# A two-layer Mamba scan kernel: a tile's finished sum leaves PSUM in one VectorE instruction behind the scan, in place of two halves around it

## The reference

```python
def step(h, inp):
    x_t, dt_t, B_t, C_t = inp
    dA = jnp.exp(dt_t[:, :, None] * A)
    h = dA * h + dt_t[:, :, None] * B_t[:, None, :] * x_t[:, :, None]
    y = jnp.einsum('bds,bs->bd', h, C_t)
    return (h, y)
...
return y * _silu(z) @ W_out
```

## Time and profile before

| | us |
|---|---|
| median of 3 runs | 2131.67 |
| profiled execution | 2132.49 |
| its span | 2130.5 |
| busy: GpSimd (POOL) | 1938.7 |
| busy: VectorE (DVE) | 1829.3 |
| busy: TensorE (PE) | 1819.0 |
| busy: ScalarE (ACT) | 1163.3 |

### The profile page before, as it was taken

The page is one execution under the profiler, slowest core; times in us unless marked ns, Lnnn a source line. Parts: engine busy times, 40 slices in busy tenths (PEclk is TensorE's granted clock), DMA queues, the critical chain, the costliest instruction groups (busy, mean ns, idle before and its releaser), DMA issues. The chain is left out here.

```text
span 2130.5 us, 16128 instructions
## 1 busy us (share of the span) xinstructions
PE 1819.0 (85%) x4474; PEld 699.1 (33%) x4474; DVE 1829.3 (86%) x1110; ACT 1163.3 (55%) x1206; POOL 1938.7 (91%) x852
## 2 busy tenths in 40 slices
PE   5798789798899899789889889879989988987777
PEld 2233233333333333233333323323333333333322
DVE  2889887877799997997898997998889999799994
ACT  2756464655755745735655744744575574453331
POOL 0999989797899999999999999899899999999996
PEclk9799899999999999999999999999999999989997
DMA  3667556555566776775675785676566677667673
GB/s 83 206 222 185 188 179 189 156 202 189 143 208 204 206 221 205 198 216 191 192 207 197 218 208 204 219 194 211 172 193 208 204 203 217 215 201 213 223 211 94
DMA packets 124454, 415.01 MB, mean 195 GB/s; under 512 B 18556, under 2 KB 22924, under 8 KB 124364
## 3 DMA queue, kind: packets, MB, share of 16 engines
q1 hardware_dynamic: 124364, 413.98, 64.5%
HBM read 403.48 MB, written 6.29 MB: 192 GB/s over the span
## 5 line engine op out<-in xcount | busy, mean ns | idle before, releaser
L861 POOL TENSOR_TENSOR ring<-ring,c_ring 128x1024 f32<-128x1024 f32 x576 | 1344.4, 2355 | 116.9 <-DVE ring L817 104.5
L495 PE MATMUL y_ps<-ring,wp 128*128 128x512 f32 x2304 | 1184.6, 629 | 79.5 <-POOL ring L861 51.0
L817 DVE TENSOR_TENSOR_SCAN ring<-a_ring,b_ps 128x1024 f32<-128x1024 f32 x392 | 895.6, 2285 | 34.1 <-ACT a_ring L624 2.5
L495 PEld LDWEIGHTS y_ps<-ring,wp 128*128 128x128 f32 x2304 | 445.2, 199 | 574.4 <-issue 387.2
L817 DVE TENSOR_TENSOR_SCAN ring<-b_ps,b_ring 128x1024 f32<-128x1024 f32 x184 | 416.6, 2272 | 52.1 <-POOL b_ring L855 24.0
L784 DVE TENSOR_TENSOR b_ps<-u_ab,b_ps 128x1024 f32<-128x1024 f32 x240 | 291.1, 1213 | 101.1 <-PE b_ps L483 88.9
L624 ACT ACTIVATE a_ring<-delta_ab,wp 128x1024 f32<-128x1024 f32 x240 | 271.8, 1140 | 176.9 <-DVE ring L817 176.3
L855 POOL TENSOR_TENSOR b_ring<-u_ab,b_ring 128x1024 f32<-128x1024 f32 x144 | 339.2, 2355 | 0.1
L617 ACT ACT_TABLE_LOAD x186 | 238.6, 1283 | 84.6 <-PE bank L518 36.4
L624 ACT ACTIVATE b_ps<-delta_ab,wp 128x1024 f32<-128x1024 f32 x144 | 160.4, 1115 | 221.2 <-DVE ring L817 220.7
L624 ACT ACTIVATE a_ring<-delta_m,wp 128x1024 f32<-128x1024 f32 x152 | 173.6, 1143 | 152.0 <-DVE ring L817 151.7
(11 more groups left out here) (75 smaller groups left out, 930.4 us busy)
## 6 DMA issues: line engine op xcount, KB each, us to landing
c_ring<-c_rows SPq DMA_DIRECT2D x384, 512.0 KB, 4.4
c_ring<-c_rows SPq DMA_DIRECT2D x384, 256.0 KB, 4.2
b_ring<-b_rows SPq DMA_DIRECT2D x144, 512.0 KB, 5.6
b_ring<-b_rows SPq DMA_DIRECT2D x80, 256.0 KB, 5.3
out<-io SPq DMA_DIRECT2D x16, 192.0 KB, 3.1
io<-x SPq DMA_DIRECT2D x6, 384.0 KB, 6.7
b_in<-parts SPq DMA_DIRECT2D x36, 64.0 KB, 2.1
dt_in<-parts SPq DMA_DIRECT2D x72, 24.0 KB
```

Source lines behind the costliest of these rows:

```text
L495: nc.tensor.matmul(half(y_ps[:, :], j), ident, half(ring[:, g % RING, :], j), start=(n == 0), stop=(n == NS - 1)).then_inc(g_summed, 1)
L817: nc.vector.tensor_tensor_scan(out=h, data0=a, data1=b, initial=0.0, op0=ALU.mult, op1=ALU.add).then_inc(h_ready, 1)
L861: nc.gpsimd.tensor_tensor(r, r, c_ring[:, g % C_RING, :], ALU.mult).then_inc(g_ready, 1)
```

## The change

VectorE's order in a step becomes scan, take, ahead, jobs. The take is one instruction over all 1024 columns, behind the scan of the fourth step of the next tile; it waits for both half-sums of the last step. y_taken counts one per tile instead of two, and its users' values follow: the first half-sum and the second half-sum of a tile's first step both wait for the whole take of the tile before. The last tile is taken in one instruction as well.

```diff
--- before.py
+++ after.py
@@ -73,7 +73,7 @@
 ACT_ORDER = ("ahead_a2", "ahead_a", "jobs")
 SP_ORDER = ("ahead_b", "ahead_c", "jobs")
 POOL_ORDER = ("ahead_b", "product", "jobs")
-DVE_ORDER = ("take_0", "scan", "take_1", "ahead", "jobs", "last")
+DVE_ORDER = ("scan", "take", "ahead", "jobs", "last")
 LEAD = {"ahead": 1, "ahead_c": C_LEAD, "ahead_a": 2, "ahead_a2": 1, "ahead_b": 3}
 SP_LEAD = dict(LEAD, ahead_b=B_LEAD)
 SUM_LAG = 3
@@ -487,7 +487,7 @@
                 n = g % NS
                 pe.wait_ge(g_ready, g + 1)
                 if n == 0:
-                    wait(pe, y_taken, 2 * (g // NS - 1) + j + 1)
+                    wait(pe, y_taken, g // NS)
                 kind, pair, k, _ = step_at(g)
                 if kind == FWD and n == SKIP_AT:
                     landed(pe, "silu", BWD, pair, 2 * k + j)
@@ -783,22 +783,21 @@
                 b = b_ps[:, g % 2, :]
                 nc.vector.tensor_tensor(b, u_of(kind, pair, k), b, ALU.mult).then_inc(b_used, 1)
 
-            def take(tile, j):
+            def take(tile):
 
                 it = ITEMS[tile // TILES]
                 kind, pair, k = it["kind"], it["pair"], tile % TILES
-                if j == 0:
-                    if kind != BWD:
-                        dve.wait_ge(K["skip_done"][kind], 3 * pair + k + 1)
-                    if kind == BWD:
-                        dve.wait_ge(y_taken, 2 * (tile - TILES + 1))
-                dve.wait_ge(g_summed, 2 * NS * (tile + 1) - 1 + j)
-                y = half(yv_of(kind, pair, k), j)
-                nc.vector.tensor_tensor(y, y, half(y_ps[:, :], j), ALU.add).then_inc(y_taken, 1)
-
-            def take_at(g, j):
+                if kind != BWD:
+                    dve.wait_ge(K["skip_done"][kind], 3 * pair + k + 1)
+                else:
+                    dve.wait_ge(y_taken, tile - TILES + 1)
+                dve.wait_ge(g_summed, 2 * NS * (tile + 1))
+                y = yv_of(kind, pair, k)
+                nc.vector.tensor_tensor(y, y, y_ps[:, :], ALU.add).then_inc(y_taken, 1)
+
+            def take_at(g):
                 if g % NS == SUM_LAG and g >= NS:
-                    take(g // NS - 1, j)
+                    take(g // NS - 1)
 
             def scan(g):
                 kind, pair, k, n = step_at(g)
@@ -819,8 +818,7 @@
 
             def take_last(g):
                 if g == ALL_STEPS - 1:
-                    for j in range(2):
-                        take(g // NS, j)
+                    take(g // NS)
 
             def job(name, kind, pair, i, unit):
                 layer = LAYER[kind]
@@ -839,7 +837,7 @@
                     nc.vector.tensor_tensor(parts3[:, i, 2, :], bank[0:SPLIT_ROWS, u % 2, :], parts3[:, i, 1, :],
                                             ALU.subtract).then_inc(evacuated[u % 2], 1)
 
-            walk(DVE_ORDER, job, ahead=look_ahead, take_0=lambda g: take_at(g, 0), take_1=lambda g: take_at(g, 1),
+            walk(DVE_ORDER, job, ahead=look_ahead, take=take_at,
                  scan=scan, last=take_last)
 
 
@@ -876,7 +874,7 @@
                     starts = d.rearrange("p (s t) -> p s t", t=W)[:, :, 0:1]
                     nc.gpsimd.memset(starts, BIG).then_inc(K["set_ready"][kind], 1)
                 elif name == "gated":
-                    pool.wait_ge(y_taken, 2 * (tile_of(kind, pair) + i + 1))
+                    pool.wait_ge(y_taken, tile_of(kind, pair) + i + 1)
                     landed(pool, "gate", ROWS if kind == ROWS else FWD, pair, 2 * i, 2 * i + 1)
                     y = yv_of(kind, pair, i)
                     nc.gpsimd.tensor_tensor(y, y, sz_of(kind, pair, i), ALU.mult).then_inc(gated_done[kind], 1)
```

## The result

| | before | after |
|---|---|---|
| median of 4 runs, us | 2132.21 | 2164.21 |
| lowest to highest | 2131.48 to 2133.13 | 2161.84 to 2167.54 |
| profiled execution, its span | 2132.49, 2130.5 | 2161.84, 2159.9 |

The ratio is 1.0151 (95% interval 1.0133 to 1.0169): 32 us slower. The sign was forecast, the size was not: 2149 was named, and the range ended at 2163. The number is near that of its first rival, TensorE's clock (2163); how much of the missing 14 us that rival accounts for, the runs bound but do not settle.

A forecast was written before the change was run, and what follows sets the result against it. No engine alone but a ring of GpSimd, VectorE and TensorE was taken as the bound. Place-by-place losses, nearly all TensorE's late half-sums, summed to 17.8 us on 2132.49 (profiled) or 2131.67 (median): 2149 named, range 2136 to 2163.

The forecast's parts named there:

- first rival, TensorE's clock: Longer TensorE standstills before first half-sums bring the low clock in 16 places, 13.8 us on top: 2163; chance 0.13.
- the ring of three engines: GpSimd, VectorE and TensorE feed each other, scan to product to sum; a pause costs time where its engine leads.
- Part 1: VectorE's own work: 0.15 us later in 23 of 35 places, nothing in 12; 3.4 us or less.
- 2.2 was written: Backward item 0, first tile: TensorE's first half-sum starts 2.2 us late behind the whole take.
- a term of 0.7: Forward item 0, first tile: 0.7 us lost through TensorE's late first half-sum.
- Part 2, the cover: TensorE's wait for the whole take: first half-sum moves to +3.75 us; B rows ready early or GpSimd's backlog hide some delays.
- Slots without a job: Takes with no TensorE job queued: 0.8 to 1.0 us late, usually covered by early B rows; 3.3 us in all.
- the remaining places: Third tiles of row and backward items, second tiles of row and forward items: nothing; 0.8 us each without cover.
- The first 500 us and forward item 0: Three early slots with jobs lose 2.8 us, forward item 0's first tile 0.7.
- Part 3: The rest: y_taken's other waits, DMA issues and the kernel's end cost nothing; 0.55 us at the end without cover.
- Rival 2: TensorE's 15% idle time swallows its delay, leaving only VectorE's 3.4 us: 2135; chance 0.11.
- Rival 3: Scans behind takes start 0.40 or 0.58 us sooner; 16 us gained if GpSimd waited for them: 2116; chance 0.06.

The follow-up runs named there:

- the wait alone: The kernel before, with one edit on TensorE: a tile's first half-sum waits for both half takes instead of half 0; 2165.29 us, ratio 1.0140.
- filling everywhere: The changed kernel, with TensorE spreading B rows five times over in the step after the take's, in every tile where it spreads them; 2157.91 us, ratio 1.0112.
- filling either half of the places: The changed kernel with B rows spread five times over only in second and third tiles (2163.69 us), or only in first tiles (2161.22 us); both ratio 1.0135.
- The extra work in third tiles: The kernel before, with B rows spread five times over (1.7 us) on TensorE in step 8 of every item's third tile, 12 times; 2141.10 us, ratio 1.0047.
- first tiles filled: The changed kernel with B rows spread five times over in the step after the take's, in first tiles only; 2161.22 us, ratio 1.0135.

## Why the prediction was wrong

- **What bounds the kernel.** Right: the ring of three engines, and the loss reaches GpSimd's wait for the scans one for one.
- **Part 1.** Where it was checked, in backward item 0's first tile, the instants are right to 0.02 us and the take's duration too (1.20 us). As a term it did not matter: the wait alone gives the whole loss.
- **The step that failed, as far as the runs show: the clock was held apart from the sum, at 0.13, and put at nothing in it.** With the clock up, the delays at two takes were near those costed: 1.8 us where 2.2 was written, 1.0 against a term of 0.7. With it down they were 3.5 and 4.4 us: the longer matmuls account for 1.7 us of the one and 3.4 of the other, and the second tile of backward item 1 fell behind by 3.9 us instead of about 1. TensorE's matmuls took 11.7 us longer in all, near the 11.6 us by which the profiled execution exceeded the sum.
  - The rival reached its 2163 by another way, one half-sum at half speed in each of 16 places. Measured were 15 takes with a low stretch near them in place of 7, some of them over jobs in a full queue. That its number came close is in part luck.
  - Both rows that the rival weighed say less than was read in them. For it: the clock at 1741 had already fallen at 1740.7, as the pause of 1.68 us began, so that pause did not bring it. Against it: a pair of matmuls at 1.10 us behind a pause does not show that the clock stays up. In forward item 0's first tile the pair behind the pause took 1.10 us in the kernel after, and the clock was at 0.51 from 433 on. At the place of the earlier trace rows itself the clock did stay at 1.00 up to 1018 us.
  - The clock's size in the whole is not settled: filling everywhere gave 6 to 8 us and may have cost some of its own, and filling either half of the places gave nothing that can be told from no change. The Trainium skill, "TensorE: Matmul & The Clock Gate", section HAM oscillation, has the rule that pauses between bursts bring the low clock; these rows agree in part, since of three pauses of 3.71 us only one did.
- **Part 2, the cover.** "Slots without a job" and the remaining places, with "Nothing" for the third tiles, came to 3.7 us in the sum; measured were 7.7 by the products and 12.9 by the scans, low clock included. The prediction judged cover by what stood right behind a place (B rows ready early, GpSimd 3 to 9 us behind). The extra work in third tiles shows that GpSimd's backlog can hide a delay and pass it on when it is used up. In the kernel after, third tile of backward item 1, the scans were up to 20.5 us late and the products 18.2; in the next item's first tile the products fell to 21.1, while the scans lost only 1.2. So most of what looks like the loss of that first tile is older, and first tiles were not clearly undersized: 10.6 predicted, 14.6 by the products, 9.3 by the scans.
  - The first 500 us and forward item 0 were put at 3.5 us: 7.0 measured, but 2.4 in the wait-alone execution. That share stays open.
- **The range.** Two thirds of 17.8 us swallowed would be 2138, not the 2136 that was written.
- **Part 3** right. **Rival 2** (slack) refuted. **Rival 3** (faster by the earlier scan) refuted: the scan did start 0.4 us earlier after its product, and the kernel was slower. The fixed cost per instruction of the Trainium skill, "Perfetto Trace Analysis", section Optimizing Scalar/DVE Operations, an estimated 4.5 us for 36 merged pairs, shows in the busy time, where VectorE's takes went from 47.9 to 43.1 us, and not in the kernel's: the engine then stood idle 27 us longer. That section's other sentence, that smaller instructions help where an engine makes others idle, agrees with the runs: 16 us between one instruction and two behind the scan.

No kernel tried beats the kernel before.

## What to carry to other kernels

Before merging two instructions that empty a buffer, ask what the first half releases: here half a take, 0.66 us long and ahead of a 2.3 us scan, let TensorE start up to 2.9 us sooner. That was worth 32 us, and the saved instruction nothing that could be measured. Where an engine must wait, put independent jobs of its queue in front of the waiting instruction, not behind it; that alone brought back 25 of 32 us. A delay hidden by another engine's backlog may only be postponed: follow it to the place where the backlog ends. And if a longer pause can lower the clock of an engine whose queue is full behind it, give that a term in the sum, even when the traces so far speak both ways.

## What was not expected of the hardware

In the first tile of backward item 0 a standstill of 2.43 us with TensorE busy on both sides was followed by a stretch at a granted clock of 0.52; with first tiles filled, with 0.70 us of pause at the same place, there was none. But the length of the pause alone does not decide. In forward item 0's first tile a pause of 2.40 us was followed by 0.51 in one kernel and one of 2.27 us by 1.00 in another. Of the three pauses of 3.71 us in the changed kernel, in second tiles of backward items, one came with the low clock and two did not. What else decides is open.

The same wait met the low clock in different places from one execution to the next: near 15 of 35 takes in the profile of the changed kernel, near 23 in that of the wait-alone run, whose span was 7.8 us longer. A pause could reach far: one of 3.71 us, with the low clock, made the six matmuls behind it take 5.46 us, against 2.81 behind a pause of the same length without it. Runs of the changed kernel spread over 5.7 us, those of the kernel before beside them over 1.7, but over 10.6 beside the first experiments, so the wider spread is not shown to be the change's.
